# Batch 0 transposed and split by halves in a gated attention block on one core

## The reference

```
xn  = layernorm(x)                                   # no gain, no bias
q, k, v = xn @ Wqkv + bqkv ; qp = elu(q)+1 ; kp = elu(k)+1
attn = (qp @ (kp^T v)) / (qp . sum(kp) + 1e-6)       # linear attention, per batch
x1  = layernorm(xn + attn) * g1 + b1
s   = layernorm(x1 + (silu(x1@Wg+bg) * (x1@Wu+bu)) @ Wd + bd) * g2 + b2
gf  = global_net(mean of xn over the tokens)         # three small layers, per batch
out = xn ; three times: out += (0.1 + 2*range*(0.7*gf + 0.3*tf(out) - 0.5)) * twist(out)
y   = x + s * silu(out)                              # tf: a four-layer net per token
```

## Time and profile before

| | |
|---|---|
| median of 3 runs | 168.56 us (168.51 to 168.8) |
| profiled execution | 168.63 us, its span 166.8 us |
| busy in the span | PE 92%, DVE 84%, ACT 75%, POOL 66% |
| chain that ended last | PE 55%, DVE 24%, ACT 8%, POOL 6%, issue 5% |
| mean granted clock of TensorE | 0.987 |

### The profile page before, as it was taken

The page is one execution under the profiler, slowest core; times in us unless marked ns, Lnnn a source line. Parts: engine busy times, 40 slices in busy tenths (PEclk is TensorE's granted clock), DMA queues, the critical chain, the costliest instruction groups (busy, mean ns, idle before and its releaser), DMA issues.

```text
span 166.8 us, 3383 instructions
## 1 busy us (share of the span) xinstructions
PE 153.5 (92%) x932; PEld 118.0 (71%) x932; DVE 139.8 (84%) x551; ACT 125.1 (75%) x319; POOL 109.4 (66%) x206
## 2 busy tenths in 40 slices
PE   5979999999999999999999999999999999999700
PEld 5657989889988786454545545788888888888700
DVE  2897699899988988599999969878698988967864
ACT  3669786999999988888887876994778687364230
POOL 0386776798973689990022175399978869679980
PEclk9999999999999999999999999999999999999995
DMA  5895222021120000000000000000001101011013
GB/s 179 257 384 133 63 65 63 0 65 37 32 63 0 2 6 0 0 0 0 4 0 0 6 0 2 0 0 4 0 2 63 63 4 65 0 63 65 4 63 126
DMA packets 11923, 7.84 MB, mean 47 GB/s; under 512 B 8960, under 2 KB 9728, under 8 KB 11904
## 3 DMA queue, kind: packets, MB, share of 16 engines
q1 hardware_dynamic: 11616, 7.55, 15.0%
q10 hardware_dynamic: 288, 0.08, 0.2%
HBM read 3.43 MB, written 2.10 MB: 33 GB/s over the span
## 4 chain that ended last, share of the span: by engine, by line
PE 55%; DVE 24%; ACT 8%; POOL 6%; issue 5%; DVEq 0%; ACTq 0%; POOLq 0%
PE bank L1135 10%; PE bank L1124 6%; PE bank L1125 6%; PE bank L1126 6%; DVE r_tok L684 5%; DVE pq L698 5%; PE bank L948 5%; DVE r_tok L687 4%; PE bank L1014 3%; PE bank L1060 2%; PE bank L1025 2%; PE bank L1005 2%; PE bank L1003 2%; PE bank L1004 2%; PE bank L965 2%
## 5 line engine op out<-in xcount | busy, mean ns | idle before, releaser
L472 ACT ACTIVATE pq<-bank,bffn 128x512 f32<-128x512 f32 (+1 forms) x24 | 16.4, 686 | 13.6 <-PE bank L1126 13.4
L259 POOL TENSOR_TENSOR rstd<-ve,minus_half 128x4 f32<-128x4 f32 (+1 forms) x25 | 24.7, 987 | 2.1
L1135 PEld LDWEIGHTS bank<-wd,pq 128*128 128x128 f32 x168 | 20.9, 191 | 1.4
L1135 PE MATMUL bank<-wd,pq 128*128 128x128 f32 x168 | 21.0, 274 | 0.0
L739 DVE SCALAR_TENSOR_TENSOR pq<-bank,bffn,pq 128x512 f32<-128x512 f32 (+1 forms) x24 | 17.5, 738 | 3.6 <-PE bank L1126 2.6
L1124 PE MATMUL bank<-x_hi,ffn_hi 128*128 128x512 f32 (+1 forms) x48 | 20.2, 421 | 0.0
L1125 PE MATMUL bank<-x_lo,ffn_hi 128*128 128x512 f32 (+1 forms) x48 | 18.9, 393 | 0.0
L1126 PE MATMUL bank<-x_hi,ffn_lo 128*128 128x512 f32 (+1 forms) x48 | 18.8, 392 | 0.0
L423 ACT ACTIVATE q_stage<-bank,col 128x512 f32<-128x512 f32 x24 | 16.3, 687 | 2.6 <-PE bank L948 1.5
L257 POOL TENSOR_SCALAR nm<-mv 128x4 f32<-128x4 f32 x23 | 5.1, 223 | 17.7 <-DVE mv L581 17.4
L1003 PE MATMUL bank<-first_hi,xT_hi 128*128 128x512 f32 x32 | 14.4, 451 | 0.0
(11 more groups left out here) (150 smaller groups left out, 437.0 us busy)
## 6 DMA issues: line engine op xcount, KB each, us to landing
x_tok<-in_x SPq DMA_DIRECT2D x8, 256.0 KB, 6.5
tx_tok<-xn_tok SPq DMA_DIRECT2D x16, 128.0 KB, 2.5
out<-pq SPq DMA_DIRECT2D x7, 256.0 KB, 2.0
r_tok<-in_w_ffn SPq DMA_DIRECT2D x1, 341.0 KB, 6.8
r_tok<-in_w_first SPq DMA_DIRECT2D x1, 320.0 KB, 3.5
out<-pq SPq DMA_DIRECT2D x2, 128.0 KB, 1.8
row<-in_rows SPq DMA_DIRECT2D x1, 192.0 KB, 6.4
wd<-in_w_down SPq DMA_DIRECT2D x1, 192.0 KB, 6.8
```

The costliest lines, as they stand in the source:

```text
L259: return pool.tensor_tensor(rstd[i][:, b, ts], ve[i][:, b, ts], minus_half[:, ts], ALU.pow)
L472: act.activation(sg[n % 2][0:m], gate_of(n)[0:m], ACT.Silu, bias=bffn[0:m, c:c + 1]).then_inc(sg_ready, 1)
L1135: last = pe.matmul(dst[:, t * P:(t + 1) * P], hid[b % 2][0:m, c, t * P:(t + 1) * P], wd[0:m, c], start=(c == 0), stop=(c == CHUNKS - 1))
```

## The change

Batch 0 is transposed into two PSUM places of 256 columns each (`ps_xT0`), with a semaphore count for each half; ScalarE (`hi_first`) and VectorE (`lo_first`) evict it by halves and leave the sums of each half in `half_sums`. VectorE adds the two halves' sums in batch 7, in front of `ctx_sum`. The subtraction for the 512 columns of weights now stands behind `lo_first(1)` on VectorE, and tile 0 waits for it only ahead of its third product; for all tiles the product with the low weights comes last. The negated mean of batch 0 is made by VectorE, and POOL makes only the other two steps of it. The aggregation of batch 1 stands ahead of `norm_first`. The memset of the constant tile is the first of all, the warm-up waits for it alone, and has 8 matmuls in place of 7.

```diff
-WARM = 7
+WARM = 8
+        sums, ctx_sum = sb("sums", [P, 2, BATCHES]), sb("ctx_sum", [P, BATCHES])
+        sum_hi, sum_lo = sums[:, 0], sums[:, 1]
+        half_sums = sb("half_sums", [P, 2, 2])
+        ps_xT0 = [bank[0][:, 0:2 * P], bank67[:, 2]]
...
-            power(0, 0).then_inc(rstd0_ready, 1)
+            pool.wait_ge(mv_ready[0], 1)
+            link(pool.tensor_scalar(ve[0][:, 0], mv[0][:, 0, :, 1], 1.0, LN_EPS, ALU.mult, ALU.add))
+            pool.tensor_tensor(rstd[0][:, 0], ve[0][:, 0], minus_half[:], ALU.pow).then_inc(rstd0_ready, 1)
...
+            def hi_first(half):
+                act.wait_ge(xT0_ps, half + 1)
+                act.activation(xT_hi[:, 0, 2 * P * half:2 * P * (half + 1)], ps_xT0[half], ACT.Identity,
+                               bias=offset[:, 0:1], accum_out=half_sums[:, half, 0:1]).then_inc(xT0_hi_ready, 1)
...
-            hi_x(0)
+            hi_first(0)
+            hi_first(1)
...
             def norm_first(b):
 
                 dve.wait_ge(rstd0_ready, 1)
+                dve.wait_ge(nm0_ready, 1)
...
+            def lo_first(half):
+                dve.wait_ge(xT0_hi_ready, half + 1)
+                cs = slice(2 * P * half, 2 * P * (half + 1))
+                ins = dve.scalar_tensor_tensor(out=xT_lo[:, 0, cs], in0=ps_xT0[half], scalar=offset[:, 0:1],
+                                               in1=xT_hi[:, 0, cs].bitcast(F32), op0=ALU.add, op1=ALU.subtract,
+                                               accum_out=half_sums[:, half, 1:2])
+                if half:
+                    ins.then_inc(xT_lo_ready, 1)
...
+            dve.memset(spread, 1.0 / (D * OFFSET)).then_inc(warm_ready, 1)
             dve.memset(minus_one[:], -1.0)
...
-            dve.memset(spread, 1.0 / (D * OFFSET))
...
             stats_x(0)
+            dve.wait_ge(mv_ready[0], 1)
+            dve.tensor_scalar(nm[0][:, 0], mv[0][:, 0, :, 0], -1.0, None, ALU.mult).then_inc(nm0_ready, 1)
             dve.wait_ge(x_loaded[1], 16)
             measure(0, 1, x_tok[:, 1])
+            moments(0, 1)
             norm_first(0)
             dve.wait_ge(first_hi_ready, 1)
             dve.tensor_tensor(first_lo[:, 4 * D:5 * D], ps_wq, first_hi[:, 4 * D:5 * D].bitcast(F32),
                               ALU.subtract).then_inc(first_ready, 1)
-            moments(0, 1)
+            lo_first(0)
+            lo_first(1)
             dve.wait_ge(first_hi_ready, 2)
             dve.tensor_tensor(first_lo[:, 0:4 * D], ps_w[:], first_hi[:, 0:4 * D].bitcast(F32),
                               ALU.subtract).then_inc(first_ready, 1)
-            lo_x(0)
...
                 if b == BATCHES - 1:
+                    dve.tensor_tensor(sums[:, :, 0], half_sums[:, 0], half_sums[:, 1], ALU.add).then_inc(sums_ready, 1)
+                    dve.wait_ge(sums_ready, 1)
                     dve.wait_ge(xT_lo_ready, BATCHES)
...
                 for t in range(TILES):
                     pe.wait_ge(xn0_ready, t + 1)
-                    last = pe.transpose(ps_xT[:, t * P:(t + 1) * P], xn_tok[:, 0, t], eye)
-                last.then_inc(xT_ps, 1)
+                    last = pe.transpose(ps_xT0[t // 2][:, t % 2 * P:(t % 2 + 1) * P], xn_tok[:, 0, t], eye)
+                    if t in (1, 3):
+                        last.then_inc(xT0_ps, 1)
...
-                pe.wait_ge(xT_hi_ready, b + 1)
                 if b == 0:
+                    pe.wait_ge(xT0_hi_ready, 2)
                     pe.wait_ge(first_ready, 1)
+                else:
+                    pe.wait_ge(xT_hi_ready, b)
...
                 if n == 0:
-                    pe.wait_ge(first_ready, 2)
+                    pe.wait_ge(first_hi_ready, 2)
...
-                pe.matmul(dst[:], hi, first_lo[:, 0:4 * D], start=False, stop=False)
-                pe.matmul(dst[:], lo, first_hi[:, 0:4 * D], start=False, stop=True).then_inc(k_ps, 1)
+                pe.matmul(dst[:], lo, first_hi[:, 0:4 * D], start=False, stop=False)
+                if n == 0:
+                    pe.wait_ge(first_ready, 2)
+                pe.matmul(dst[:], hi, first_lo[:, 0:4 * D], start=False, stop=True).then_inc(k_ps, 1)
...
+            pe.wait_ge(warm_ready, 1)
+            warm_up(WARM)
             pe.wait_ge(consts_ready, 1)
-            warm_up(WARM)
```

More of the change, by code:

```diff
@@ L141, in gated_block @@
         rden = sb("rden", [P, BATCHES, TILES])
-        sum_hi, sum_lo, ctx_sum = sb("sum_hi", [P, BATCHES]), sb("sum_lo", [P, BATCHES]), sb("ctx_sum", [P, BATCHES])
+        sums, ctx_sum = sb("sums", [P, 2, BATCHES]), sb("ctx_sum", [P, BATCHES])
+        sum_hi, sum_lo = sums[:, 0], sums[:, 1]
+        half_sums = sb("half_sums", [P, 2, 2])
         gh1, gh2, gt = sb("gh1", [P, BATCHES]), sb("gh2", [P, BATCHES]), sb("gt", [P, BATCHES])
@@ L177, in gated_block @@
         ffn_hi_ready, pool_const, cols_ready, consts_ready = sem("ffn_hi_ready"), sem("pool_const"), sem("cols_ready"), sem("consts_ready")
+        warm_ready, nm0_ready, xT0_ps, xT0_hi_ready, sums_ready = [
+            sem(n) for n in ("warm_ready", "nm0_ready", "xT0_ps", "xT0_hi_ready", "sums_ready")]
         centre_ready, shifted_ready, diag_ready, w_ps, rstd0_ready = [
@@ L370, in hi_x @@
             def hi_x(b):
-                act.wait_ge(xT_ps, b + 1)
+                act.wait_ge(xT_ps, b)
                 if b >= 2:
@@ L602, in norm_first @@
                                       rstd[0][:, b, t:t + 1], ALU.add, ALU.mult).then_inc(xn0_ready, 1)
+            def lo_first(half):
[6 more added lines that the diff above has]
+                    ins.then_inc(xT_lo_ready, 1)
             def lo_x(b):
-                dve.wait_ge(xT_hi_ready, b + 1)
+                dve.wait_ge(xT_hi_ready, b)
                 if b >= 2:
@@ L853, in _ @@
                 if b == BATCHES - 1:
+                    dve.tensor_tensor(sums[:, :, 0], half_sums[:, 0], half_sums[:, 1], ALU.add).then_inc(sums_ready, 1)
+                    dve.wait_ge(sums_ready, 1)
                     dve.wait_ge(xT_lo_ready, BATCHES)
-                    dve.scalar_tensor_tensor(out=ctx_sum[:], in0=sum_hi[:], scalar=-OFFSET * SEQ, in1=sum_lo[:],
+                    dve.scalar_tensor_tensor(out=ctx_sum[:], in0=sum_hi, scalar=-OFFSET * SEQ, in1=sum_lo,
                                              op0=ALU.add, op1=ALU.add).then_inc(ctx_ready, 1)
```

## The result

The changed kernel takes 169.20 us (median of 20 runs, 168.85 to 169.89), the kernel before beside it 168.69 us (20 runs, 168.46 to 169.39). The ratio is 1.0024 with a 95% interval of 1.0014 to 1.0034: slower by 0.24%, some 0.4 us, against a forecast of 169.0 us. The profiled execution took 169.08 us with a span of 167.3, against 168.63 and 166.8.

What follows compares the result with a forecast made beforehand. TensorE heads the chain; its start is a relay between engines, and VectorE's queue is late next. Batch 0's 0.08 plus batch 7's 0.38 make 0.46; 168.63 becomes 169.09, less 0.07 for the median: 169.0 us, range 168.2 to 169.3.

Steps and rivals of the forecast that it cites:

- Batch 0, +0.08: Start of the kernel: the exponential comes earlier, but VectorE's longer queue makes feature_k(0) and sum_kv(0) later, +0.08 us.
- the head start: Batch 0: the first exponential starts 0.54 us earlier, at 10.00, a lead forecast to end in VectorE's queue.
- rival (a): Batch 0: ScalarE's chain, not VectorE's queue, holds feature_k(0), so sum_kv(0) comes 0.54 earlier: 168.2 to 168.4; chance 0.20.
- Batch 7, +0.38: Batch 7: the added addition waits for POOL, then ctx_sum waits for POOL's next instruction; copy_kv(6) is 0.38 us later.
- Rival (c): Batch 7: ctx_sum misses the second wait for the port, 0.08 + 0.18, 168.8 us; chance 0.09.
- Rival (e): Batch 7: its delay is hidden because something else is as late, +0.08, 168.6 us; chance 0.08.
- The part on two-port modes: Batch 0: VectorE's little copies and scalings might wait for POOL's normalisation of batch 1, up to 0.2 more, 169.2.
- The sum: Whole kernel: batch 0's 0.08 plus batch 7's 0.38 make 0.46 us slower.
- (b): Start: TensorE's clock rises with the earlier warm-up, near 4.8; -0.15 at batch 0, +0.23 in all, 168.8; chance 0.11.
- (d): Start: idle time in front of the centring costs the clock's rise, up to 1.4 more, about 170.4; chance 0.05.
- the gain of 0.23: Batch 0: with the mean made by VectorE, POOL's power ends earlier and norm_first starts at 6.61, 0.23 us gained.

Runs made afterwards that it cites:

- before + addition: Kernel before with an unused two-element VectorE addition, and a wait for it, ahead of ctx_sum in batch 7: 169.33 us, ratio 1.0026.
- warm-up of 9: Kernel after with 9 warm-up matmuls in place of 8: 169.06 us, ratio 1.0026.
- ctx_sum late: Kernel of "statistics spread" with ctx_sum and its waits moved behind feature_k(31), the last of batch 7: 167.66 us, ratio 0.9939.
- statistics spread: Kernel of "sum early" with half of batch 2's statistics moved behind feature_k(0) and their moments behind feature_k(1) on VectorE: 168.37 us, ratio 0.9976.
- After, again: Kernel after, unchanged, measured once more for a second profile: 169.55 us, ratio 1.0038.
- sum early: Kernel after with the addition of the half sums moved from batch 7 to batch 0 on VectorE: 169.16 us, ratio 1.0007.

## Why the prediction was right

**Batch 0, +0.08.** Measured +0.05 at sum_kv(0). The steps stand within a tenth: norm_first 6.65 (forecast 6.61), evictions 7.93 and 8.39 (7.90, 8.37), the subtraction 9.40 (9.40), the exponential 10.07 (10.00), copies 10.00 (9.98), feature_q 11.56 (11.54), feature_k(0) 12.13 (12.14), sum_kv(0) 12.46 (12.49). TensorE's gap ahead of it reads 0.36 in the profile, not 0.6; counted from 11.94, where one more matmul would have started at the pace of those before it, it is 0.52. That VectorE's queue ends the head start is shown, not only argued: cutting either of two unlike pieces out of the queue brings the whole 0.5 back, and rival (a), the head start kept, came true in those kernels. How much of the 0.47 came from the halves and how much from the earlier norm_first was not taken apart.

**Batch 7, +0.38.** Measured 2.70 to 3.07, so +0.37, and 3.06 or 3.07 in every trace that has the addition there, the kernel before with it among them; it is gone in every trace that has not. Rival (c), the second wait missed, is out: ctx_sum lasted 0.34 each time and met POOL's next instruction. Rival (e) is out by "before + addition", 1.0026. Rows 6, the same sequence elsewhere in the trace, were the right evidence to take the dearer end.

The rule behind the repeated wait is in the Trainium skill, "SBUF — State Buffer", Who interferes with whom: a VectorE instruction with both inputs in SBUF contends with a GpSimd instruction that reads SBUF. The traces agree behind POOL's longer instructions: ctx_sum and coupling(0), 8 elements each, last 0.58 to 0.63 behind the 1.3 us of L300 (L295 in the kernel before) and end within 0.03 of it, where coupling(0) has its short outcome. They do not agree for every instruction of POOL: ctx_sum lasted 0.16 in the midst of the power L264, which reads SBUF too. The part on two-port modes, which I carried as up to 0.2 more, is not seen: the copies and scalings began at 10.00, 10.12, 10.18 and on by 0.06, as before, while POOL's normalisation L269 ran until 10.23 beside the first of them. That is a short overlap of instructions with one element per partition, no proof for longer or larger ones.

**The sum.** 0.46 forecast, 0.45 measured in the profiled executions and 0.4 by the ratio. The absolute time was 0.2 low: the job that timed both kernels put the kernel before at 168.69, 0.13 above the median that I started from. That the sum agrees this closely is partly luck. The two profiled executions happened to have nearly the same rise of the clock (5.53 and 5.71) and the same coupling(0) (0.60 and 0.61), and the kernel after measured again gave 1.0038, some 0.6 us.

**The clock, rivals (b) and (d).** Both tied the rise to the warm-up's start or to the gap behind it. Neither holds. With the new warm-up (start near 1.04) the rise came at 4.4 to 7.3, with the old one (near 1.7) at 4.7 to 7.6. The latest two, 7.46 and 7.61, are from kernels without a gap behind the warm-up, and closing the gap (warm-up of 9) changed neither the time nor its spread. The rule of the Trainium skill that I weighed, "TensorE: Matmul & The Clock Gate", Part 1, that what the chip watches runs freely and is not reset by the kernel's start, agrees with these fourteen traces. Of the sizes named, that of (b) was right: in "warm-up of 9", with an early rise, the first eviction starts at 7.66 (7.64 in the rival), feature_k(0) at 11.91 (11.9) and sum_kv(0) at 12.24, 0.2 earlier than in the kernel after. That of (d), up to 1.4, was too large: in the second trace of the kernel before, with the rise at 7.46, the weights' cast starts 0.9 later (7.42 to 8.32) and sum_kv(0) 0.4. A late rise moves the cast L514 past 8.1, as here in "ctx_sum late", TensorE and ScalarE:

```profile
1.05 3.78 PE L1000 MATMUL bank<-r_tok 128*128 128x128 f32 x16 [1.05 <-DVE r_tok L837]
...
5.82 1.43 PE L992 MATMUL bank<-r_tok 128*128 128x384 f32 x2
...
8.16 0.58 ACT L514 CAST first_hi<-bank 128x512 fp32r<-128x512 f32 x1 [0.38 <-PE bank L995]
```

Two passes of 384 columns take 1.43 in place of 0.81, and sum_kv(0) comes at 12.66, where the sibling with the early rise had 11.67. That 1.0 us is as large as the spread between runs of one kernel, and it is the main thing that a single profile of this kernel can mislead by. It may also be why the times of "statistics spread" lie in two groups, eight at 168.09 to 168.39 and four at 168.99 to 169.31; only one execution of each kernel is traced, so this is not shown.

**What I missed.** First, the price of norm_first's new place. The statistics of batch 1 stood ahead of it before, but it waited for POOL's rstd (1.16 to 1.43 us behind the start of these statistics in four traces). With the moments of batch 1 ahead of it too, it starts 1.20 to 1.21 behind them in all ten traces with the new order: it hangs on the landing of batch 1's data. "After, again", VectorE and POOL:

```profile
5.95 0.88 DVE L588 BATCH_NORM_STATS2 st<-x_tok 128x6 f32<-128x128 f32 x4 [0.76 <-DMA x_tok<-in_x]
6.86 0.38 DVE L594 BATCH_NORM_AGGREGATE mv<-st 128x2 f32<-128x6 f32 x4
7.16 1.08 DVE L615 TENSOR_SCALAR xn_tok<-x_tok,nm,rstd 128x128 f32<-128x128 f32 x4
...
5.51 1.01 POOL L342 TENSOR_TENSOR rstd<-ve,minus_half 128x4 f32<-128x4 f32 x1
```

rstd was there at 6.52, but the data had landed 0.5 us later than in the first trace, and norm_first went from 6.65 to 7.16. In the kernels with the old order it stayed at 6.74 to 6.89, with statistics that started at 5.33 to 5.63. So the gain of 0.23 that I booked for POOL's shorter list was 0.19 in one execution and -0.3 in another. The -0.3 is the four aggregations (0.29): with data as late as this, the old order would have had to wait for the statistics too, until an estimated 6.83 (5.95 and 0.88). Second, the race near 69 us: rows 6 held the very place, and I read it for a price but not for a second outcome, 0.60 or 0.95 to 0.99, that hides or feigns 0.25 to 0.4 us in any comparison of single traces. What decides between the two was not found.

## What to carry to other kernels

A head start won in a relay must be followed through the queue of every engine that feeds the next wait of an in-order TensorE: here 0.47 us arrived at one engine and none left the other, and cutting that queue elsewhere brought it back. Look along the critical engine for tiny instructions with two SBUF inputs at places where POOL runs long instructions back to back: one that waits costs as much as an eviction (0.6 us for 8 elements), and two in a row cost 0.8 us (2.26 against 3.07) where they take 0.15 and 0.16 elsewhere. Moving one away gave the lowest time of this study, but most of that gain arose at another such place, because POOL came ahead there: compare the whole trace, not only the place of the edit. And don't add work behind a transfer and ahead of the critical instruction because it fits on the average.

## What the runs showed of the hardware that I had not expected

- A VectorE instruction that waits for POOL does not surely come next when POOL's instruction ends. In "sum early" coupling(0) started 0.54 us ahead of POOL's L306 (69.12 against 69.66), and ended with it at 70.07. The same program shows 0.60 in one execution and 0.99 in another; here the second of the kernel before, whose first is in the earlier trace rows:

```profile
69.47 0.99 DVE L670 SCALAR_TENSOR_TENSOR cpl<-tt,gain,base 128x8 f32<-128x8 f32 x1 [1.96 <-ACT tt L444]
```

- Such an instruction does not wait for POOL at all times that POOL is busy. It lasted 0.58 to 0.63 behind POOL's 1.3 us on 512 columns, 0.34 behind 0.42 us on 256 columns, 0.23 and 0.29 beside instructions of 0.45 us on 128 columns, and 0.16 in the midst of POOL's power of 1.01 us on 4 columns.

- Where the clock rises varies from 4.42 to 7.61 us over fourteen traces of kernels that give TensorE nearly the same work up to there. A rise near 7 lengthened sum_kv(0)'s arrival by 0.4 us in the kernel before (12.41 to 12.84) and by 1.0 between "statistics spread" and "ctx_sum late", where less else stands in its way. The granted clock of the profile does not show this: it reads 1.00 over 4 to 9 us in traces that have passes of both durations there. Read the durations:

```profile
4.00:9.00 5.00, 4.55 (x18) 3.14 (x17) 3.71 (x22) 2.90 (x8) 2.98 (x7) 1.00 0.98 261
```

That is the stretch 4 to 9 of "ctx_sum late": its length, busy time and count of TensorE, its weight loads, VectorE, ScalarE and POOL, then the granted clock, the share of the DMA engines and GB/s. The rise in that trace is at 7.06.
